# A layer norm moved behind the projections: raw x1 multiplied with column-centred attention weights, in a one-core perceiver block

## The reference, cut to what matters

```python
_layernorm(x) = (x - mean(x)) / sqrt(var(x) + 1e-5)        # over the 256 features

x = x + cross_attention(ctx, _layernorm(x))                # 12544 context rows, 128 queries, softmax over queries
# attention with 16 heads of 16, causal:
qkv = _layernorm(x) @ w_attn + b_attn ; q, k, v = split(qkv)
att = softmax(where(causal, q @ k.T / 4, -inf)) ; y = att @ v
x = x + y @ w_proj + b_proj
x = x + _layernorm(x) @ W.T + b + (_layernorm(x) @ V_r) @ C.T
```

## Time and profile before

| | us |
|---|---|
| runs | 106.11, 105.77, 106.12 (median 106.11) |
| the profiled execution | 105.76 |
| its span, first to last instruction | 103.7 |
| TensorE busy | 98.3 (95% of the span) |
| VectorE / ScalarE / GpSimd busy | 76.3 / 72.7 / 63.8 |
| read from memory | 27.59 MB |
| granted TensorE clock, mean | 0.998 |

### The profile page before, as it was taken

The page is one execution under the profiler, slowest core; times in us unless marked ns, Lnnn a source line. Parts: engine busy times, 40 slices in busy tenths (PEclk is TensorE's granted clock), DMA queues, the critical chain, the costliest instruction groups (busy, mean ns, idle before and its releaser), DMA issues.

```text
span 103.7 us, 2257 instructions
## 1 busy us (share of the span) xinstructions
PE 98.3 (95%) x740; PEld 86.4 (83%) x740; DVE 76.3 (74%) x217; ACT 72.7 (70%) x268; POOL 63.8 (62%) x46
## 2 busy tenths in 40 slices
PE   5999999999999999999999999999999999969990
PEld 1389999999999999999999999999998976845660
DVE  0412959959999999988777797777889745699641
ACT  4019599599999999997777977778879304489410
POOL 6405499869999999999766797666886001004020
PEclk9999999999999999999999999999999999999999
DMA  3899999999999999999999999993000000000001
GB/s 70 330 417 412 411 411 406 408 408 408 414 400 409 403 416 406 408 409 409 408 406 406 411 408 409 388 369 125 0 0 6 0 0 0 0 0 0 6 0 51
DMA packets 8746, 27.86 MB, mean 269 GB/s; under 512 B 1120, under 2 KB 1824, under 8 KB 8736
## 3 DMA queue, kind: packets, MB, share of 16 engines
q1 hardware_dynamic: 8736, 27.73, 68.3%
HBM read 27.59 MB, written 0.13 MB: 267 GB/s over the span
## 4 chain that ended last, share of the span: by engine, by line
PE 89%; DVE 4%; DMA 2%; issue 1%; POOL 1%; ACT 0%; DVEq 0%
PE bank L323 43%; PE bank L335 21%; PE bank L338 10%; DVE head_max L716 2%; DMA x<-x_dram 2%; PE bank L406 2%; PE bank L443 1%; PE bank L344 1%; PE bank L419 1%; PE bank L500 1%; PE bank L308 1%; PE bank L486 1%; PE bank L389 1%; PE bank L386 1%; PE bank L462 1%
## 5 line engine op out<-in xcount | busy, mean ns | idle before, releaser
L288 POOL TENSOR_TENSOR rows_split<-rows_ring,rows_split 128x1024 fp32r<-128x1024 f32 (+1 forms) x25 | 58.4, 2335 | 16.9 <-ACT rows_split L518 16.8
L323 PE MATMUL bank<-query_t,cols_ring 128*128 128x128 f32 x392 | 47.5, 276 | 0.0
L323 PEld LDWEIGHTS bank<-query_t,cols_ring 128*128 128x128 f32 x392 | 45.7, 192 | 1.3 <-ACT query_t L509 0.3
L529 ACT ACTIVATE bank<-bank,neg_max 128x128 f32<-128x128 f32 x98 | 33.1, 338 | 7.4 <-DVE neg_max L653 7.2
L335 PE MATMUL bank<-rows_split,probs 128*128 128x512 f32 x92 | 34.7, 413 | 0.0
L518 ACT CAST rows_split<-rows_ring 128x1024 fp32r<-128x1024 f32 (+1 forms) x25 | 25.8, 1033 | 6.1 <-DMA rows_ring<-ctx_rows_dram 5.1
L670 DVE SCALAR_TENSOR_TENSOR probs<-bank,inv_sums,probs 128x128 fp32r<-128x128 f32 x98 | 27.6, 345 | 0.9
L338 PE MATMUL bank<-rows_split,probs 128*128 128x256 f32 x92 | 25.6, 279 | 0.0
L653 DVE TENSOR_REDUCE neg_max<-bank 128x4 f32<-128x512 f32 (+1 forms) x25 | 16.8, 672 | 8.6 <-PE bank L323 8.6
L335 PEld LDWEIGHTS bank<-rows_split,probs 128*128 128x128 f32 x92 | 17.3, 189 | 3.1
L529 ACT ACTIVATION_READ_ACCUMULATOR bank<-bank,neg_max 128x1 f32 x98 | 19.8, 202 | 0.0
(11 more groups left out here) (96 smaller groups left out, 64.0 us busy)
## 6 DMA issues: line engine op xcount, KB each, us to landing
cols_ring<-ctx_cols_dram SPq DMA_DIRECT2D x24, 512.0 KB, 14.8
rows_ring<-ctx_rows_dram SPq DMA_DIRECT2D x24, 512.0 KB, 15.2
wqk_sb<-w_qk_dram SPq DMA_DIRECT2D x1, 512.0 KB, 11.6
cols_ring<-ctx_cols_dram SPq DMA_DIRECT2D x1, 256.0 KB, 11.3
rows_ring<-ctx_rows_dram SPq DMA_DIRECT2D x1, 256.0 KB, 12.1
wv_sb<-w_v_dram SPq DMA_DIRECT2D x1, 256.0 KB, 11.7
wproj_sb<-w_proj_dram SPq DMA_DIRECT2D x1, 256.0 KB, 10.4
wffn_sb<-w_ffn_dram SPq DMA_DIRECT2D x1, 256.0 KB, 9.7
```

What stands on the lines that cost most here:

```text
L288: pool.tensor_tensor(rows_split[:, b, 0:n, 1, :], rows_ring[:, slot * STEP:slot * STEP + n, :], rows_split[:, b, 0:n, 0, :].bitcast(F32), ...
L323: last = pe.matmul(into[:, t * P:(t + 1) * P], cols_ring[:, slot * STEP + t, c, :], query_t[:, c, :], start=(c == 0), stop=(c == DC - 1))
L529: last = act.activation(on[:, t * P:(t + 1) * P], on[:, t * P:(t + 1) * P], ACT.Exp, bias=neg_max[:, b, t:t + 1], accum_out=sums[:, b, t:t ...
```

## The change: what it does

In words, by engine:

- SyncE: `w_qk` and `w_v` leave the list behind the stream and are loaded behind step 11 and step 13; a transposed copy of all attention weights `w_t` (128 x 6 x 256 floats, 0.79 MB) is loaded behind step 9.
- VectorE, in the stream: three reductions of `w_t` (128 x 512 to 128 x 2) behind steps 8, 9 and 10, and the negated means (128 x 6) behind step 11.
- ScalarE issues two transfers: behind step 12 the store of the 768 means to memory, element by element, and behind step 19 their load, spread over 128 partitions (128 x 768).
- GpSimd adds the means to the weights in place, six additions of 128 x 256: two behind steps 22 and 23, four behind step 24.
- The tail: x1 is formed in two halves and transposed raw; both halves are copied by ScalarE. `rstd` is multiplied onto the identity (VectorE), a product with a matrix of ones spreads it over the partitions (`rstd_wide_ps`, TensorE, in its own part of bank 6), ScalarE copies it. Projections k0, q0, k1, q1 are multiplied by it out of PSUM (`scaled`, VectorE, four instructions). The keys' two writes per half are shared by ScalarE and GpSimd, one query half is written by ScalarE and one by VectorE. The values are scaled by `rstd` as they get their bias, in four instructions in place of two.
- W is added to the low-rank product by GpSimd, not by two multiplications; `x1_bias` moves from VectorE to GpSimd; the masks of score banks 0 and 1 are multiplied behind the projections.

```diff
@@ sync
+                if s == WT_AT:                       # 9
+                    sp.dma_start(wt_sb[:], w_t).then_inc(wt_landed, 16)
+                if s == WT_AT + 2:
+                    sp.dma_start(wqk_sb[:], w_qk).then_inc(wqkv_landed, 16)
+                if s == WT_AT + 4:
+                    sp.dma_start(wv_sb[:], w_v).then_inc(wqkv_landed, 16)
@@ gpsimd
+            def centre_weights(n):
+                pool.wait_ge(means_landed, 16)
+                pool.wait_ge(wqkv_landed, 32)
+                part = wqk_sb[:, :, n, :] if n < 2 * DC else wv_sb[:, :, (n - 2 * DC) * P:(n - 2 * DC + 1) * P]
+                pool.tensor_tensor(part, part, means_wide[:, n, :].unsqueeze(1).to_broadcast([P, DC, P]),
+                                   ALU.add).then_inc(wqkv_centred, 1)
...
             inverse_std(1)
+            pool.wait_ge(diag_ready, 1)
+            pool.tensor_tensor(x1_bias[:], x1[:], bproj_sb[:], ALU.add).then_inc(x1_bias_ready, 1)
+            for c in range(DC):
+                pool.wait_ge(scaled_ready, 2 * c + 1)
+                pool.tensor_scalar(k_t[:, c, 1, :], scaled[:, DC + c, :], bqk_sb[:, DC + c:DC + c + 1], parity[:, 1:2],
+                                   ALU.add, ALU.mult).then_inc(k_copied[c], 1)
+            pool.wait_ge(low_rank_copied, 1)
+            pool.wait_ge(q_copied[1], 1)
+            pool.tensor_tensor(wffn_sb..., wffn_sb..., low_rank[:], ALU.add).then_inc(wffn_ready, 1)
@@ tensor
+            multiply_low_rank(0)
             for c in range(DC):
+                pe.wait_ge(x1_ready, c + 1)
+                pe.transpose(turn[c][:, 0:P], x1[:, c * P:(c + 1) * P], ident[:]).then_inc(turned, 1)
+            multiply_low_rank(1).then_inc(low_rank_ready, 1)
+            pe.wait_ge(wqkv_centred, 3 * DC)
             pe.wait_ge(turn_copied_first, 2)
             for n in [DC, 0, DC + 1, 1]:
+                if n == DC + 1:
+                    pe.wait_ge(diag_ready, 1)
+                    pe.wait_ge(ones_ready, 1)
+                    pe.matmul(rstd_wide_ps, ones[:], rstd_diag[:], start=True, stop=True).then_inc(rstd_spread, 1)
+                    pe.wait_ge(low_rank_copied, 1)
                 if n == 1:
-                    pe.wait_ge(wffn_ready, 1)
+                    pe.wait_ge(rstd_copied, 1)
...
+            mask_scores(0)
+            mask_scores(1)
@@ scalar
+                if s == STORE_AT:                    # 12
+                    act.wait_ge(neg_means_ready, 1)
+                    act.dma_start(col_means.rearrange("o (n p) -> p (o n)", p=P), neg_means[:],
+                                  allow_slow_non_contiguous=True).then_inc(means_stored, 16)
+                if s == FETCH_AT:                    # 19
+                    act.wait_ge(means_stored, 16)
+                    act.dma_start(means_wide[:].rearrange("p n d -> p (n d)"), col_means.to_broadcast([P, 3 * D]))\
+                       .then_inc(means_landed, 16)
...
+            act.wait_ge(rstd_spread, 1)
+            act.copy(rstd_wide[:], rstd_wide_ps).then_inc(rstd_copied, 1)
+            finish_keys(0)           # k_t[:, 0, 0, :] from scaled, bias and scale per partition
+            act.wait_ge(scaled_ready, 2)
+            act.activation(q_t[:, 0, :], scaled[:, 0, :], ACT.Identity, bias=bq_scaled[:, 0:1], scale=SCALE)
+            finish_keys(1)
@@ vector
+            def sum_columns(third):
+                dve.wait_ge(wt_landed, 16)
+                part = slice(third * DC, (third + 1) * DC)
+                dve.tensor_reduce(col_sums[:, part], wt_sb[:, part, :], AX_X, ALU.add).then_inc(sums_ready, 1)
...
+            statistics(x1[:])
+            dve.wait_ge(rstd_ready, 2)
+            dve.tensor_scalar(rstd_diag[:], ident[:], rstd[:, 0:1], None, ALU.mult).then_inc(diag_ready, 1)
+            dve.wait_ge(rstd_copied, 1)
             for c in range(DC):
                 dve.wait_ge(k_ready, c + 1)
+                dve.tensor_tensor(scaled[:, DC + c, :], k_ps[c][:, 0:P], rstd_wide[:], ALU.mult)
+                dve.wait_ge(q_ready, c + 1)
+                dve.tensor_tensor(scaled[:, c, :], q_ps[c][:, 0:P], rstd_wide[:], ALU.mult)
+            dve.wait_ge(scaled_ready, 2 * DC)
+            dve.tensor_scalar(q_t[:, 1, :], scaled[:, 1, :], SCALE, bq_scaled[:, 1:2], ALU.mult, ALU.add)
...
             for e in range(2):
-                dve.tensor_tensor(v_pad[:, :, e, :, e * HD:(e + 1) * HD], v_view[:, :, e], bv_view[:, :, e], ALU.add)
+                for c in range(DC):
+                    dve.scalar_tensor_tensor(v_pad[:, c, e, :, e * HD:(e + 1) * HD], v_view[:, c, e], rstd[:, 0:1],
+                                             bv_view[:, c, e], ALU.mult, ALU.add).then_inc(v_copied, 1)
```

More of the change, by code:

```diff
@@ L32 @@
 ENDING = 2
+WT_AT = 9
+SUMS_AT = 8
+STORE_AT, FETCH_AT = 12, 19
+CENTRE_AT, CENTRED = 22, 2
 def perceiver_kernel(nc, x, ctx_rows, ctx_cols, w_qk, b_qk, w_v, b_v, w_proj, b_proj,
-                     w_ffn, b_ffn, v_r, c_t, out):
+                     w_ffn, b_ffn, v_r, c_t, w_t, col_means, out):
     T, D = x.shape
@@ L104, in perceiver_kernel @@
         ct_sb = sb("ct_sb", [R, D])
+        wt_sb = sb("wt_sb", [P, 3 * DC, D])
+        col_sums = sb("col_sums", [P, 3 * DC])
+        neg_means = sb("neg_means", [P, 3 * DC])
+        means_wide = sb("means_wide", [P, 3 * DC, P])
+        ones = sb("ones", [P, P])
+        rstd_diag = sb("rstd_diag", [P, P])
+        rstd_wide = sb("rstd_wide", [P, P])
+        scaled = sb("scaled", [P, 2 * DC, P])
+        bk_parity = sb("bk_parity", [P, DC, 2])
+        low_rank = sb("low_rank", [P, DC * D])
         q_t = sb("q_t", [P, DC, P])
@@ L175, in perceiver_kernel @@
         v_ready = sem("v_ready")
-        q_copied = sem("q_copied")
-        k_copied = sem("k_copied")
+        wt_landed = sem("wt_landed")
+        wqkv_landed = sem("wqkv_landed")
+        sums_ready = sem("sums_ready")
+        neg_means_ready = sem("neg_means_ready")
+        means_stored = sem("means_stored")
+        means_landed = sem("means_landed")
+        wqkv_centred = sem("wqkv_centred")
+        ones_ready = sem("ones_ready")
+        diag_ready = sem("diag_ready")
+        rstd_spread = sem("rstd_spread")
+        rstd_copied = sem("rstd_copied")
+        scaled_ready = sem("scaled_ready")
+        bk_parity_ready = sem("bk_parity_ready")
+        low_rank_copied = sem("low_rank_copied")
+        q_copied = [sem(f"q_copied{c}") for c in range(DC)]
+        k_copied = [sem(f"k_copied{c}") for c in range(DC)]
         parity_ready = sem("parity_ready")
@@ L204, in perceiver_kernel @@
         out_stored = sem("out_stored")
-        weights = [(wqk_sb, w_qk), (bqk_sb, b_qk), (wv_sb, w_v), (bv_sb, b_v.to_broadcast([P, D])),
+        weights = [(bqk_sb, b_qk), (bv_sb, b_v.to_broadcast([P, D])),
                    (wproj_sb, w_proj), (bproj_sb, b_proj.to_broadcast([P, D])), (wffn_sb, w_ffn), (bffn_sb, b_ffn.to_broadcast([P, D])),
@@ L562, in _ @@
                .then_inc(x1_bias_centred_ready, 1)
[L564 to L568, removed]
             def exps_by_head(j):
@@ L612, in link, with statistics @@
                 dve.wait_ge(dve_step, link_count[0])
-            def layer_norm(n, src):
+            def statistics(src):
                 link(dve.bn_stats(bn[:, 0:6], src))
                 dve.bn_aggr(mean_var[:], bn[:]).then_inc(stats_ready, 1)
[L617 to L629, removed]
             dve.memset(warm[:], 0.0).then_inc(warm_ready, 1)
+            dve.memset(ones[:], 1.0).then_inc(ones_ready, 1)
             dve.memset(bn[:, 6:8], 0.0).then_inc(eps_ready, 1)
@@ L636, in _ @@
             dve.wait_ge(x_landed, 16)
-            layer_norm(0, x0[:])
-            copy_turn(0, query_t)
+            statistics(x0[:])
+            dve.wait_ge(stats_ready, 1)
+            dve.wait_ge(rstd_ready, 1)
+            for c in range(DC):
+                half = slice(c * P, (c + 1) * P)
+                dve.tensor_scalar(normed[:, half], x0[:, half], mean_var[:, 0:1], rstd[:, 0:1],
+                                  ALU.subtract, ALU.mult).then_inc(normed_ready, 1)
+            dve.wait_ge(turned, DC)
+            dve.tensor_copy(query_t[:, 1, :], turn[1][:, 0:P]).then_inc(turn_copied, 1)
             def invert(s):
@@ L740, in _ @@
             for e in range(2):
-                dve.tensor_tensor(v_pad[:, :, e, :, e * HD:(e + 1) * HD], v_view[:, :, e], bv_view[:, :, e],
-                                  ALU.add).then_inc(v_copied, 1)
+                for c in range(DC):
+                    dve.scalar_tensor_tensor(v_pad[:, c, e, :, e * HD:(e + 1) * HD], v_view[:, c, e], rstd[:, 0:1],
+                                             bv_view[:, c, e], ALU.mult, ALU.add).then_inc(v_copied, 1)
             copy_exp_t(0)
```

78 lines of the change are left out of this document (50 added, 28 removed).

## The result

The changed kernel takes 108.28 us (median, 107.91 to 110.14) against 106.05 (105.77 to 106.46) for the kernel before: a ratio of 1.021, interval 1.0188 to 1.0232. The prediction was 105.5 us with a range to 107.1. Run again on another chip, unaltered, it took 108.78 against 105.95: 1.0274 (1.0237 to 1.0311). The traces shown here of the changed kernel are of that second run; in the first, TensorE's granted clock fell near the end, which lengthened the span to 108.4 us.

A forecast was written before the change was run, and what follows sets the result against it. TensorE bounds the stream at 3.18 us a step; the tail is one chain. Scores 0.8 us earlier less 0.15 for the values gives 0.65 off the 106.11 median: 105.5 us, range 104.9 to 107.1.

The forecast's parts named there:

- the sum for the store: Stream, steps 16 to 19: 768 pieces at up to 0.087 us cost 2 us, at most 4.2, within the columns' margins.
- The margin of 4.6 us: Stream, step 19: its columns would still land 4.6 us before use, after 3.84 us of delay by early weights.
- margins of 2.6 to 3.9 us: Stream: probabilities keep 2.6 us at step 8, about 2.7 and 3.3 at 10 and 12; 3.9 for ScalarE's issuing.
- Rival two: Stream starves: TensorE waits for columns between steps 10 and 20; net +1.0, 107.1 us; chance 0.20 together with rival three.
- Rival three: Tail: GpSimd late for the power as its additions wait for the means; some 1 us, folded into rival two's 0.20.
- Early loads, sums, additions: Stream: TensorE never waits, by 0.9 us; three reductions of 0.68 each and six GpSimd additions of 0.73 each fit.
- The negation of 128x6: Stream, behind step 11: by the skill's rule it would wait for one GpSimd subtraction, thinning a 3.3 us margin.
- The tail: Behind the stream: scores 0.8 us earlier, 0.15 given back on the values, a gain of 0.65 us to the end.
- From x1 to the scores: Tail: scores start at 88.35 to 88.45 in place of 89.21, a gain of 0.8 us.
- The values' four instructions: Tail, VectorE: four 128x64 instructions take 0.72 us, +0.24, of which 0.15 counts to the end.
- GpSimd's key writes: Tail: GpSimd's part of k0 taken at 0.45 us; at 0.73 the scores would start 0.1 later.

The follow-up runs named there:

- 24-byte kernel: The changed kernel with its 768 means stored in 128 pieces of 24 bytes in place of 768 of 4 bytes; 105.4 us, ratio to before 0.9949.

## Why the prediction was wrong

**The step that failed** is the sum for the store: "the store is 4.2 us of every engine, my upper end. I take 2 us", and from it "even 4.2 us, spread over these as they come, just passes". Both the size and what it was set against were wrong.

The size: 6.8 us were lost, 4 x (31 + 315 + 236) / 408 = 5.7 of them before step 19 is scored. The load of step 19's columns landed 6.2 us later than in the 24-byte kernel (22.2 us behind its issue and not 16.0), 5.4 in the first trace. The margin of 4.6 us that I had put there was right: the 24-byte kernel has 4.8. So step 19 is where TensorE waits, 2.2 us late in one trace and 0.5 in the other.

What it was set against: the columns alone. For the probabilities I had reckoned margins of 2.6 to 3.9 us around these steps, and I held only ScalarE's time for issuing the store against them, not the late rows. By that path TensorE waited 0.8 us in the last steps in one trace and 1.6 in the other, and x1 was 3.3 to 3.5 us late in both.

Rival two was right in mechanism and place, as far as the columns go; I gave it 0.20 together with three. I priced it at +1.0 where the kernel lost 2.2 to 2.8.

The price came from `bqk_sb`, a load. The load of 768 pieces here lost 0.4 us, so for reading even 4.2 was far too much. For the packed store it was too little, since its cost isn't one for each piece. A row of another direction and another layout was no bound, though it was the nearest there was. I named the rule of the Trainium skill (DMA: Bandwidth & Descriptors, Specifications) that below 512 B the engine reads, modifies and writes, and gave it no chance of its own. The trace agrees with a cost of writing small pieces, but not with one that every piece below 512 B has: 4 bytes cost nothing 64 bytes apart.

**Rival three** I folded away: GpSimd "would need to slip 2.4 us" and had "9 us" for the means. It slipped not by the means, which had landed at 78.1 (issued at 70.6, 7.5 us to landing) and were first added at 81.4, but by the late rows, which it splits in the same queue, and was 0.5 us late for the power. The cover was measured against the kernel's own pace, and failed when the stream did.

**Early loads, sums, additions.** Right: with 24-byte pieces TensorE has no wait in the stream. The six additions take 0.73 each as put, 0.87 with strided means. The negation of 128x6 took 1.17 us. In the 24-byte kernel it runs from 43.76 to 44.95, GpSimd's subtraction from 42.55 to 44.93. That fits the Trainium skill (SBUF — State Buffer, Who interferes with whom), as I had written it: VectorE's instruction ends 0.02 us behind GpSimd's. It stayed in the margin.

**The tail.** Right in kind, 0.40 us in place of 0.65 (x1 to the last write, by the spans, in the 24-byte kernel). Two terms were off. From x1 to the scores I had 0.8, it is 0.56: TensorE's first low-rank product delays the transposes, and the spread waits until q0 has gone in at 86.84, 2.44 us behind x1 where I had 2.33; ScalarE's writes from `scaled` take 0.39 to 0.49, not 0.35. The values' four instructions take 0.85, not 0.72, and all of the 0.37 us beyond the old 0.48 is on the path, where I counted 0.15. GpSimd's key writes took 0.88 for two, 0.45 each as taken.

**The forecast 105.5** is what the 24-byte kernel measures (105.4): the estimate was one for a kernel whose store does no harm. That the number fits so well is in part luck, since the trace of that kernel shows 0.40 us and not 0.65 in the tail.

## What to carry to other kernels

A transfer that nothing waits for still takes the queues from those that are waited for: ask what it takes from them, against the smallest margin in the 20 us behind it, and read GB/s, not the engines' busy share. Set the disturbance against every chain that the transfers feed, here the probabilities as well as the columns. Write to memory so that one partition's values lie together in one piece (24-byte pieces did no harm), or pad them apart; choose the layout for the store and let an engine read the result with a step. A term whose nearest row is of another kind is unbounded, and belongs in the chance of the rival, not in the sum.

## What the runs showed of the hardware that I had not expected

- 128 packed 4-byte writes from 128 partitions, 512 bytes in all, take 7.0 us of transfers away from a stream of 408 GB/s. 256 and 768 take 7.2 and 6.1. 768 writes 64 or 256 bytes apart take 0.0, 768 reads 0.4. Why the packed ones hold the other queue up stays open.
- The DMA busy share doesn't follow the bytes: in windows of 4 us it was 1.17 at 145 GB/s, 1.29 at 113 and 0.64 at 138, against 1.03 at 409.
- Beside a full stream, whose own loads take 14 to 16 us, a store on ScalarE's queue lands in 7.0 us (128 pieces of 24 bytes), 12.6 and 13.1 us (768 pieces of 4 bytes, 64 and 256 bytes apart) or 18.2 us (768 packed).
- In the kernel with 128 packed pieces added, TensorE was busy for 1.46 of 2 us in the tail, and then its granted clock averaged 0.56 and 0.59 for 4 us; the projections there took 3.69 us in place of 2.39.
